# Graph network kernel, last stage: finishing tiles of nodes beside the last gathers, with their products ahead of each group's own matmuls

## What is computed

```python
feature = x1 - mean(x1, axis=0)
feature = feature / (std(x1, axis=0, ddof=1) + 0.0001)
support = segment_sum(edge_weight[:, None] * feature[src], dst, num_segments=N)
out = layernorm(x1 + support @ weight + bias, axis=-1)
```

## Time and profile before

| what | us |
|---|---|
| median of three runs | 4497.64 (4493.88 to 4502.54) |
| span of the profiled execution | 3538.9 |
| median less span | 958.7 |
| last stage, from POOL's start (about 2369) to the last addition | about 1116 |
| closing part, 3485.24 to 3538.9 | 53.7 |

### The profile page before, as it was taken

How to read it: one execution, slowest core, us unless ns; L and a number is a source line. 1 busy time by engine, 2 the same in 40 slices (tenths; PEclk the granted TensorE clock), 3 DMA queues, 4 the chain that set the end, 5 groups by cost and what they waited for, 6 DMA issues and landing times.

```text
span 3538.9 us, 60836 instructions
## 1 busy us (share of the span) xinstructions
PE 2637.8 (75%) x13420; PEld 2074.9 (59%) x13420; DVE 2160.9 (61%) x5264; ACT 1014.6 (29%) x3087; POOL 2575.7 (73%) x2754
## 2 busy tenths in 40 slices
PE   5667777777777777799999999967666655565657
PEld 4455555545555455588888886435555555555556
DVE  7977854444444444377777766875565666666656
ACT  3343333333333323255555554640000000000003
POOL 6777677777777777777777765767777777777772
PEclk8887798999989989899999999988788777777678
DMA  6556566666666666589999986543333333333333
GB/s 173 155 152 208 164 215 208 209 209 206 207 210 210 211 203 212 175 283 291 294 293 296 291 273 198 158 155 105 105 106 103 105 105 105 105 105 105 105 105 108
DMA packets 317352, 639.37 MB, mean 181 GB/s; under 512 B 56776, under 2 KB 135054, under 8 KB 317131
## 3 DMA queue, kind: packets, MB, share of 16 engines
q0 software_dynamic: 122112, 335.31, 30.1%
q1 hardware_dynamic: 192410, 298.20, 27.6%
q10 hardware_dynamic: 2608, 3.40, 0.3%
HBM read 479.98 MB, written 156.69 MB: 180 GB/s over the span
## 4 chain that ended last, share of the span: by engine, by line
PE 30%; POOL 28%; issue 17%; DMA 11%; DVE 8%; DVEq 2%; ACT 2%; SPq 1%; ACTq 0%; POOLq 0%
PE ps L1053 11%; POOL columns L572 10%; POOL work L572 9%; PE ps L879 8%; POOL messages L529 8%; DMA messages<-work,stage 4%; PE ps L1114 3%; PE ps L995 3%; DMA work<-place_row 3%; DMA columns<-x_table,wh 2%; POOL work L510 2%; PE ps L1078 2%; DMA work<-in_x,stage 2%; PE ps L1153 1%; DMA work<-x_table,wh 1%
## 5 line engine op out<-in xcount | busy, mean ns | idle before, releaser
L510 POOL DMA_INDIRECT work<-in_x,stage x832 | 790.6, 950 | 291.6 <-issue 226.6
L529 POOL DMA_INDIRECT messages<-work,stage x832 | 801.2, 963 | 265.4 <-issue 237.5
L995 PE MATMUL ps<-work 128*128 128x256 f32 x1664 | 478.5, 438 | 260.9 <-DVE work L1638 257.3
L1971 DVE TENSOR_TENSOR node_a<-node_a,ps 128x256 f32 x880 | 370.1, 421 | 414.5 <-PE ps L1114 213.8
L879 PE MATMUL ps<-work 128*128 128x128 f32 x3328 | 464.8, 299 | 145.2 <-ACT work L621 104.6
L995 PEld LDWEIGHTS ps<-work 128*128 128x128 f32 x1664 | 346.2, 217 | 382.7 <-DVE work L1638 170.4
L879 PEld LDWEIGHTS ps<-work 128*128 128x128 f32 x3328 | 443.1, 212 | 211.5 <-ACT work L621 134.0
L572 POOL DMA_INDIRECT columns<-x_table,wh x480 | 457.9, 954 | 146.2 <-issue 138.9
L683 ACT ACTIVATE work<-ps,columns 128x256 f32<-128x256 f32 x832 | 325.8, 474 | 708.7 <-PE ps L995 692.4
L1114 PE MATMUL ps<-work,columns 128*128 128x128 f32 x1920 | 346.1, 354 | 232.1 <-DMA columns<-x_table,wh 232.0
L1114 PEld LDWEIGHTS ps<-work,columns 128*128 128x128 f32 x1920 | 318.0, 259 | 281.1 <-DMA columns<-x_table,wh 281.1
(11 more groups left out here) (275 smaller groups left out, 3208.1 us busy)
## 6 DMA issues: line engine op xcount, KB each, us to landing
work<-messages SPq DMA_DIRECT2D x232, 520.0 KB
work<-place_row SPq DMA_DIRECT2D x208, 256.0 KB, 4.0
work<-in_x SPq DMA_DIRECT2D x256, 128.0 KB, 3.0
gate_rows<-work SPq DMA_DIRECT2D x49, 384.0 KB, 2.4
columns<-gate_rows SPq DMA_DIRECT2D x49, 384.0 KB, 3.0
work<-in_x,stage POOLq DMA_INDIRECT x832
messages<-work,stage POOLq DMA_INDIRECT x832, 3.3
messages<-zeros SPq DMA_DIRECT2D x50, 260.0 KB
```

The lines of the kernel that those rows point to most:

```text
L510: nc.gpsimd.indirect_dma_start(out=big[:, s, j, 0:D], out_offset=None, in_=table, in_offset=bass.IndirectOffsetOnAxis(ap=stage[:, s, j:j + ...
L529: nc.gpsimd.indirect_dma_start(out=messages, out_offset=bass.IndirectOffsetOnAxis(ap=stage[:, s, j:j + 1], axis=0), in_=big[:, s, j, :], i ...
L995: last = nc.tensor.matmul(b[:, (j % 2) * D:(j % 2 + 1) * D], hots[:, j * P:(j + 1) * P], tab[:, h, :], start=True, stop=True)
L1971: last = V.tensor_tensor(tile_of(node_a, w), tile_of(node_a, w), ps[2 * (g % LAST_SUMS) + k // 2][:, (k % 2) * D:(k % 2 + 1) * D], ALU.add)
```

## The change

A tile is now finished while gathers still run. `whole_by(t)` is the last group that can hold a chunk of tile t. PE issues the tile's product two groups behind that, ahead of that group's own matmuls; DVE adds it one group later, at the head of its turn, and puts the tile's `bn_stats` and `bn_aggr` between the group's additions. The products have banks 6 and 7 alone, four halves. The one-hots of the group five ahead, which stood before a group's additions, now stand between them one by one, in the whole stage. `result` moves from the work area, where the gathered rows lie, to the buffer of the weights `wx`, which is free by then. Tiles that are whole too late are finished behind the last group as before.

```diff
@@ -31,6 +31,7 @@
 LAST_SUMS = 3
 NCH = -(-(E // P + NT) // (4 * CPG)) * 4 * CPG
 DEST_BITS = 10
+FIRST_END = E // P
 EPS = 1e-5
 
 F32 = mybir.dt.float32
@@ -211,7 +212,7 @@
         ub, gb = area(2048, [2, 2 * D]), area(3072, [2, 2 * D])
         st = area(hot_at, [2, 4, P])
         node_rows = area(hot_at + 2048, [2, D])
-        result = area(0, [2 * RING, D])
+        result = wx[:, :, :].rearrange("p k (u d) -> p (k u) d", d=D)
         xn, hn = area(hot_at + 1024, [2, D]), area(hot_at + 1536, [2, D])
 
         shifted = area(hot_at + 1024, [2, 2 * D])
@@ -282,6 +283,16 @@
         X_SHIFT = 1 + XPAIRS // RING
         PREP = RANKED
         BATCHES = -(-NT // RING)
+
+        def final_sum(t):
+            return ps[6 + t // 2 % 2][:, t % 2 * D:(t % 2 + 1) * D]
+
+        def whole_by(t):
+
+            return (FIRST_END + t) // CPG
+
+        def finals_of(g, lag):
+            return [t for t in range(NT) if min(whole_by(t) + lag, LAST) == g]
 
         def batch(b):
             return range(b * RING, min((b + 1) * RING, NT))
@@ -1101,10 +1112,12 @@
                 nc.tensor.matmul(ps[7][:, 0:D], ones[0:TAIL, :], shifted[0:TAIL, s, 0:D], start=False, stop=True).then_inc(S["x1_sq_used"], 1)
 
 
-            def second_turn(i, after=None):
+            def second_turn(i, after=None, before=None):
                 for s in range(RING):
                     g = RING * i + s
                     k, h = g % LAST_ROWS, g % LAST_HOTS
+                    if before:
+                        before(i, s)
 
                     pe.wait_ge(S[f"second_rows{k}"], (g // LAST_ROWS + 1) * 16 * CPG)
                     pe.wait_ge(S["second_hot"], g + 1)
@@ -1141,17 +1154,23 @@
             for k in range(2):
                 last = nc.tensor.matmul(ps[7][:, 0:D], mean_t[:, k, :], w1[:, k, :], start=k == 0, stop=k == 1)
             last.then_inc(S["shift_mm"], 1)
+
+            def final(t):
+
+                pe.wait_ge(S["second_added"], whole_by(t) + 1)
+                if t >= 4 and t % 2 == 0:
+                    pe.wait_ge(S["e_y"], NT + t - 2)
+                for k in range(2):
+                    last = nc.tensor.matmul(final_sum(t), node_a[:, t, k * P:(k + 1) * P], w1[:, k, :], start=k == 0, stop=k == 1)
+                last.then_inc(S["e_mm"], 1)
+
+            def finals(i, s):
+                for t in finals_of(RING * i + s, 2):
+                    final(t)
             for i in range(SQUARED + 4, LAST_TURNS):
-                second_turn(i)
-
-
-            pe.wait_ge(S["second_done"], 1)
-            for t in range(NT):
-                if t >= 8:
-                    pe.wait_ge(S["e_y"], NT + t - 7)
-                for k in range(2):
-                    last = nc.tensor.matmul(ps[t % 8][:, 0:D], node_a[:, t, k * P:(k + 1) * P], w1[:, k, :], start=k == 0, stop=k == 1)
-                last.then_inc(S["e_mm"], 1)
+                second_turn(i, before=finals)
+            for t in finals_of(LAST, 2):
+                final(t)
 
 
         @block.vector
@@ -1955,35 +1974,75 @@
                     V.scalar_tensor_tensor(o, mean_b[:, :], node_c[:, bass.ds(t + u, 1), D + 1], o, ALU.mult, ALU.add).then_inc(S["x1_biased"], 1)
 
 
-            def hot_second(g):
-
-                need(dve, S["second_mm"], g - LAST_HOTS + 1)
-                for j in range(CPG):
-                    last = V.tensor_scalar(last_hot[g % LAST_HOTS][:, j, :], iota[:, :], back[:, g * CPG + j:g * CPG + j + 1, 1],
-                                           back[:, g * CPG + j:g * CPG + j + 1, 0], ALU.is_equal, ALU.mult)
-                last.then_inc(S["second_hot"], 1)
-
-            def add_second(g, wins):
-
-                dve.wait_ge(S["second_mm"], g + 1)
-                for k, w in enumerate(wins):
-                    need(dve, S["second_adds"], g * CPG + k)
-                    last = V.tensor_tensor(tile_of(node_a, w), tile_of(node_a, w),
-                                           ps[2 * (g % LAST_SUMS) + k // 2][:, (k % 2) * D:(k % 2 + 1) * D], ALU.add)
-                    last.then_inc(S["second_adds"], 1)
-                dve.wait_ge(S["second_adds"], (g + 1) * CPG)
-                dve.sem_inc(S["second_added"], 1)
+            def last_scale(b):
+                ts = slice(batch(b)[0], batch(b)[-1] + 1)
+                dve.wait_ge(S["l_dev"], b + 1)
+                dve.sem_inc(S["may"], 1)
+                link(V.reciprocal(rstd_all[:, ts], rstd_all[:, ts]))
+                V.scalar_tensor_tensor(neg_mean[:, ts], mv_all[:, ts, 0], -1.0, rstd_all[:, ts], ALU.mult, ALU.mult).then_inc(S["l_rstd"], 1)
+
+            def final_add(t):
+
+                dve.wait_ge(S["e_mm"], NT + min(t // 2 * 2 + 2, NT))
+                V.tensor_tensor(node_c[:, t, 0:D], node_c[:, t, 0:D], final_sum(t), ALU.add).then_inc(S["e_y"], 1)
+
+            def final_stats(t):
+
+                dve.wait_ge(S["e_y"], NT + t + 1)
+                dve.wait_ge(S["e_mv"], NT + t - 1)
+                V.bn_stats(bn6[:, t % 2, :], node_c[:, t, 0:D]).then_inc(S["e_bn"], 1)
+
+            def final_mean_var(t):
+
+                dve.wait_ge(S["e_bn"], NT + t + 1)
+                dve.sem_inc(S["may"], 1)
+                V.bn_aggr(mv_all[:, t, :], bn6[:, t % 2, :]).then_inc(S["e_mv"], 1)
+
+            def scales_of(g):
+
+                return [b for b in range(BATCHES) if batch(b)[-1] in finals_of(g - 1, 3)]
+
+
+            def hot_second(g, j):
+
+                if j == 0:
+                    need(dve, S["second_mm"], g - LAST_HOTS + 1)
+                hot_j = V.tensor_scalar(last_hot[g % LAST_HOTS][:, j, :], iota[:, :], back[:, g * CPG + j:g * CPG + j + 1, 1],
+                                        back[:, g * CPG + j:g * CPG + j + 1, 0], ALU.is_equal, ALU.mult)
+                if j == CPG - 1:
+                    hot_j.then_inc(S["second_hot"], 1)
+
+            def add_second(g, j, w):
+
+                need(dve, S["second_adds"], g * CPG + j)
+                V.tensor_tensor(tile_of(node_a, w), tile_of(node_a, w),
+                                ps[2 * (g % LAST_SUMS) + j // 2][:, (j % 2) * D:(j % 2 + 1) * D], ALU.add).then_inc(S["second_adds"], 1)
 
             def second_turn(i):
                 for g in range(RING * i, RING * (i + 1)):
-                    if g + LAST_HOTS - 1 < LAST:
-                        hot_second(g + LAST_HOTS - 1)
-                    add_second(g, windows(g, range(CPG), chunk_wins))
+                    ts = finals_of(g, 3)
+                    for t in ts:
+                        final_add(t)
+                    wins = windows(g, range(CPG), chunk_wins)
+                    dve.wait_ge(S["second_mm"], g + 1)
+                    for j in range(CPG):
+                        add_second(g, j, wins[j])
+                        if j < len(ts):
+                            final_stats(ts[j])
+                        if g + LAST_HOTS - 1 < LAST:
+                            hot_second(g + LAST_HOTS - 1, j)
+                        if j < len(ts):
+                            final_mean_var(ts[j])
+                    dve.wait_ge(S["second_adds"], (g + 1) * CPG)
+                    dve.sem_inc(S["second_added"], 1)
+                    for b in scales_of(g):
+                        last_scale(b)
 
 
             dve.wait_ge(S["back_kept"], 2 * PAIRS)
             for g in range(LAST_HOTS - 1):
-                hot_second(g)
+                for j in range(CPG):
+                    hot_second(g, j)
 
             dve.wait_ge(S["in_cleared"], NT)
             link(V.memset(in_sums[:, :, NT * P:NTP * P], 0.0))
@@ -2013,36 +2072,25 @@
                 add_shift(2 * (i - SHIFTS), 2)
                 second_turn(i)
             add_shift(FULL, 1)
-            for i in range(SHIFTS + FULL // 2, LAST_TURNS - 1):
+            dve.wait_ge(S["x1_biased"], 3 * (FULL // 2) + 2)
+            for i in range(SHIFTS + FULL // 2, LAST_TURNS):
                 second_turn(i)
-            second_turn(LAST_TURNS - 1)
-            dve.wait_ge(S["x1_biased"], 3 * (FULL // 2) + 2)
-            dve.sem_inc(S["second_done"], 1)
-
-
-            def last_scale(b):
-                ts = slice(batch(b)[0], batch(b)[-1] + 1)
-                dve.wait_ge(S["l_dev"], b + 1)
-                dve.sem_inc(S["may"], 1)
-                link(V.reciprocal(rstd_all[:, ts], rstd_all[:, ts]))
-                V.scalar_tensor_tensor(neg_mean[:, ts], mv_all[:, ts, 0], -1.0, rstd_all[:, ts], ALU.mult, ALU.mult).then_inc(S["l_rstd"], 1)
-
-            for t in range(NT + 5):
-                if t < NT:
-                    dve.wait_ge(S["e_mm"], NT + t + 1)
-                    V.tensor_tensor(node_c[:, t, 0:D], node_c[:, t, 0:D], ps[t % 8][:, 0:D], ALU.add).then_inc(S["e_y"], 1)
-                if 0 <= t - 1 < NT:
-                    dve.wait_ge(S["e_y"], NT + t)
-                    dve.wait_ge(S["e_mv"], NT + t - 2)
-                    V.bn_stats(bn6[:, (t - 1) % 2, :], node_c[:, t - 1, 0:D]).then_inc(S["e_bn"], 1)
```

(24 more changed lines are left out.)

## The result

The changed kernel takes 4564.62 us (median of 4 runs) against 4495.76: 68.9 us or 1.59% slower (ratio 1.0159, 95% interval 1.0133 to 1.0184). The forecast was 4544.9, 47.3 us slower, range 4524 to 4570.

The account below looks back on a forecast made before the run. Gathers bound the kernel until 3480 us, 4.98 a group. Turn 210 at 10.5, nine PE-DVE turns of 13.46 and 18.1 for the rest end the span 47.3 later: 4497.64 + 47.3 = 4544.9 us, range 4524 to 4570.

Parts of the forecast that it names:

- The loop: Turns 211 to 219: PE's products wait for DVE's additions, DVE waits for matmuls behind them; almost no overlap, 13.46 us a turn.
- the rival in which DVE alone is the bound: Final turns: PE and DVE overlap after all, 6.34 us a turn, 22 us faster, 4476; chance 0.08.
- (a): Start of a turn: two final additions on DVE until PE starts, 0.99 us.
- (b): PE's four products in a turn, 0.865 us each at full clock: 3.46 us.
- (d): PE's clock in each turn: a burst starting after a pause loses 1.60 us.
- (c): The group's matmuls in a turn, from start to DVE's first addition at full clock: 2.43 us.
- (e): DVE's four steps in a turn, each an addition, bn_stats, a one-hot and bn_aggr: 4.72 us.
- (f): Scale of a batch in a turn, DVE's reciprocal to the next addition: 0.26 us.
- The rival of half speed throughout: Final turns: PE stays at half speed, 16.6 us a turn, 81 us slower, 4579; chance 0.07.
- The closing part: Behind group 219: seven products, the clock's loss and the old kernel's tail, 17.1 us from the first product.
- the 958.7 us between the span and the median I leave as they are: Whole kernel: span 3538.9 against median 4497.64; the difference was kept unchanged because the number of instructions hardly changes.
- What was costed at nothing: One-hots moved in all turns, undelayed gathers, output stores, ACT's normalising and the result buffer's new place: no cost.

Follow-up runs that it names:

- both ways of opening it: Changed kernel with each group's products issued behind its own matmuls, 0.9999 of the kernel before; or with eight half banks for the products instead of four, 1.0013.
- the products behind: Changed kernel with the four products of a group issued behind the group's own matmuls instead of ahead: 0.9999 of the kernel before.
- with the scales spread: Changed kernel with products behind the group's matmuls and, in the closing loop, each batch scaled soon after its last tile: 0.9984 of the kernel before.
- the one-hots (1.0008): Kernel before with only the one-hots moved between a group's additions in all 220 turns, tiles finished at the end as before: ratio 1.0008.

## Why the prediction was right, point by point

**The loop** is as described: shown by the two waits on each other above and by both ways of opening it, which bring the turn from 13.6 us to between 6.2 and 6.4. That is near the 6.34 of the rival in which DVE alone is the bound.

**The terms of one turn**, forecast and measured in the turn from 4434.61 to 4448.50. (a) Final additions to PE's start: 0.99, measured 0.89 (4447.61 to 4448.50). (b) and (d), products with the clock: 5.06, measured 5.77 (4434.61 to 4440.38), 5.4 to 5.7 in later turns; so the clock costs about 2.0 us a burst and not 1.60. (c) Group to first addition: 2.43, measured 2.17. (e) Four steps: 4.72, measured 4.77 (4442.55 to 4447.32); statistics to aggregate 0.58 for 0.59, aggregate to the next addition 0.28 for 0.25. (f) 0.26, measured 0.29. Together 13.89 for 13.46. The rival of half speed throughout falls: the group's own matmuls, 1.95 us from 4440.38, have a granted clock of 1.00. (Its support, "pauses of about 3 us", was read too simply: PE's waits in the earlier trace rows are 3.08, 3.07 and 1.38 us.)

**The stage**, in the executions without pauses. From group 209's matmuls to turn 211's burst I had 17.8 us (3430.17 to 3448.0); it took 14.4. Nine turns 123.6 for 121.1. The closing part 22.7 for 17.1: I had carried over the end of the kernel before, where each batch is scaled within the loop, and overlooked that the changed loop leaves batches 9 to 12 until after the last tile. Together that is 4.7 us more than forecast. That the two spans still differ by 48.1 and not by 52 is no merit of the sum: in these runs the kernel before also took 1.5 us more from group 209 on than in the profile I had (110.2 for 108.7), and began that group 2.5 us later than the changed kernel.

**The rest of the 68.9.** The step that failed is "the 958.7 us between the span and the median I leave as they are". They are not outside the program but pauses within it, and they change the base. After the last pause the kernel before starts its last ten groups 3.75 us apart and not 4.98, so PE reaches group 219 11 us sooner. DVE's additions come behind, so only half of that counts: from group 210 to the first closing product it takes 44.9 us (4336.16 to 4381.07), and in the profile read for the prediction 50.2, from this row to 3485.24:

```profile
3435.03 3.44 PE L1114 MATMUL ps<-work 128*128 128x128 f32 x16 [1.93 <-DMA work<-x_table,wh]
```

That is 5.3 us less in which to hide anything. Counted from the end of that pause, the kernel before needs 99.8 us (4336.16 to 4436.0) and the changed kernel, which still has group 209 (3.75) before it, 165.1 (4386.58 to 4551.7): 61.6 more, a little below the 63 to 76 measured on the changed kernel's chip (the two profiles are from different chips). The remaining 9 us or so would lie ahead of that point; that the pauses bring them is argued, not shown. Nor can these profiles show it: two kernels that differ only behind group 219, the products behind without and with the scales spread, take 1269.6 (3056.9 to 4326.51) and 1285.3 us (3079.1 to 4364.38) from the first gather to group 209.

The products behind fare by the same base, but it doesn't explain all. From group 210 to the end they gain 17.7 us on the kernel before without pauses (87.4 against 105.1) and 9.9 with them (89.9 against 99.8). In the timed runs with pauses nothing is left of the 9.9 (0.9999, at best 7 us faster); where it goes is open.

So the forecast holds for its mechanism and its turn, and the 4564.62 lies in the range by luck. The room above 4544.9 was meant for longer steps and a slower clock, worth 2.5 us over nine turns in all; what filled it was the changed base, the batches left to the end, and some 9 us that nobody has placed.

**What was costed at nothing** held as far as can be told: the one-hots (1.0008), and the gathers without pauses (POOL's last gather at 3479.3 in the changed kernel, 3482.1 in the kernel before).

**The clock.** Stage rows (as the earlier trace rows) of the changed kernel, the two halves of a burst of four products that starts after a pause of 6.14 us:

```profile
4489.72:4492.50 2.78, 2.78 (x7) 2.25 (x8) 0.51 (x2) 1.59 (x4) 0.00 (x0) 0.50 0.16 55
4492.50:4495.24 2.74, 2.74 (x11) 2.30 (x10) 0.00 (x0) 0.00 (x0) 0.00 (x0) 0.77 0.41 139
```

and a whole burst with the products behind, after a pause of 0.87 us:

```profile
4396.89:4400.42 3.53, 3.53 (x17) 3.12 (x18) 3.03 (x10) 1.60 (x4) 0.00 (x0) 1.00 0.33 115
```

The granted clock stands at the lower level (0.50, that is 1.2 GHz) for the first half and comes back in the second. After pauses of 6.14 to 6.51 us the four products take 5.4 to 5.7 us up to the group's start, after pauses of 0.87 to 1.24 us 3.5. The rule of the Trainium skill (TensorE: Matmul & The Clock Gate, Part 1) that PE falls to its lower clock when it idles agrees with each of these turns.

## What to carry to other kernels

When late work is moved into a loop of two engines, ask of its first wait: who clears it, and is that engine itself waiting for something that stands behind the moved work in this queue? Full buffers on the input side (eleven here) didn't help; one more turn's worth of result buffers, or placing the moved work behind the loop's own, does, and either halved the turn here. And compare a profile's span with the timed runs before summing against it: where they differ by a fifth, it shows an engine slack that the timed runs may not have.

## What the hardware showed that I hadn't expected

The same program, the kernel before, takes 3550.78 us on one chip and 4433.39 or 4476.37 on two others (medians of 7, 29 and 17 runs); its clock's mean is 0.87 to 0.88 there and 0.80 to 0.81 on the others. POOL's busy time is the same in both kinds of execution (2575.7 and 2575.2 us), and its gathers take the same 946 ns (median). But the last stage's gathers stretch from 1107 us (2370.2 to 3477.3) to 1288 (3051.8 to 4340.2), with pauses of PE of some 10 us. In the one that ends at 4336.16, PE waits for DVE, DVE's additions come 2.1 to 3.5 us apart where 0.71 is usual, and POOL stops once for 3.73 us on an unknown queue:

```profile
4329.97 0.42 DVE L1971 TENSOR_TENSOR node_a<-node_a,ps 128x256 f32 x1 [2.44 <-issue]
...
4333.44 0.42 DVE L1971 TENSOR_TENSOR node_a<-node_a,ps 128x256 f32 x1 [3.05 <-issue]
```

What DVE and POOL wait for there, nothing in the profile names, and it was not found. Each profile's span lies 1.7 to 1.8 us below its own run, where I could compare them, in both kinds of execution.
